# Scatter-adding weighted expert rows into the residual in memory, with gathers six blocks ahead and a copy at the end

## The reference

```python
x = L0_attn_x                                   # 8 x 512 x 512
x = x + 0.5 * ffn(layernorm(x))
x = x + attention(layernorm(x))                 # 16 heads, ALiBi bias, causal
x = x + 0.5 * ffn(layernorm(x))

def ffn(h, gate, up, down, topk_idx, topk_weight):   # E = 32 experts, K = 4 per token
    perm = argsort(topk_idx.reshape(-1))
    tok = repeat(arange(n), K)[perm]
    g, u = ragged_dot(h[tok], gate), ragged_dot(h[tok], up)
    o = ragged_dot(silu(g) * u, down) * topk_weight.reshape(-1)[perm][:, None]
    return zeros(n, 512).at[tok].add(o)
```

## Time and profile before

| | |
|---|---|
| median of 3 runs | 3252.62 us (3252.36 to 3259.63) |
| profiled execution, its own time | 3253.32 us |
| span of the trace | 3251.6 us |
| busy share of the span | PE 83%, PE weight load 60%, DVE 50%, ACT 40%, POOL 34% |
| moved by transfers | 434.78 MB, 134 GB/s over the span |

### The profile page before, as it was taken

How to read it: one execution, slowest core, us unless ns; L and a number is a source line. 1 busy time by engine, 2 the same in 40 slices (tenths; PEclk the granted TensorE clock), 3 DMA queues, 4 the chain that set the end, 5 groups by cost and what they waited for, 6 DMA issues and landing times. The chain is left out here.

```text
span 3251.6 us, 65525 instructions
## 1 busy us (share of the span) xinstructions
PE 2698.2 (83%) x13668; PEld 1963.3 (60%) x13669; DVE 1631.8 (50%) x3136; ACT 1306.9 (40%) x3316; POOL 1089.8 (34%) x1529
## 2 busy tenths in 40 slices
PE   1259999999992799999899999986899999999800
PEld 0148887888881455555555555553788788888700
DVE  8754444544433364654646465542444445454245
ACT  1235555555542222322322232221555555555422
POOL 2435555555541000100110001001455555455456
PEclk9999999999996788888897888886999999999955
DMA  2335444455403344343434434320455455543088
GB/s 71 129 123 173 163 160 154 173 175 173 151 13 116 94 112 118 98 129 93 130 93 122 114 91 127 79 79 36 154 175 172 150 167 173 178 158 110 1 322 298
DMA packets 153904, 434.78 MB, mean 134 GB/s; under 512 B 30993, under 2 KB 32529, under 8 KB 141538
## 3 DMA queue, kind: packets, MB, share of 16 engines
q1 hardware_dynamic: 95520, 282.25, 27.9%
q0 software_dynamic: 55936, 151.10, 13.9%
q10 hardware_dynamic: 2370, 0.64, 0.1%
HBM read 290.10 MB, written 125.83 MB: 128 GB/s over the span
## 5 line engine op out<-in xcount | busy, mean ns | idle before, releaser
L430 PE MATMUL f_psg<-f_wh,f_xh 128*128 x1280 | 563.5, 440 | 17.0 <-DVE f_idle L575 9.1
L430 PE MATMUL f_psg<-f_wh,f_xl 128*128 x1280 | 505.8, 395 | 0.0
L430 PE MATMUL f_psg<-f_wl,f_xh 128*128 x1280 | 504.1, 394 | 0.0
L380 POOL DMA_INDIRECT f_xg<-xn_rows,f_it x320 | 337.4, 1054 | 264.9 <-POOL f_it L377 264.0
L388 POOL DMA_INDIRECT y_rows<-f_ob,f_ip x320 | 329.5, 1030 | 284.6 <-POOL f_ip L385 253.3
L1219 DVE TENSOR_REDUCE a_mx<-a_psa 128x1 f32<-128x128 f32 (+3 forms) x512 | 237.6, 488 | 243.4 <-PE a_psa L983 234.6
L569 DVE TENSOR_TENSOR f_wl<-f_wraw,f_wh 128x768 f32 x256 | 244.9, 959 | 200.0 <-ACT f_wh L494 199.9
L582 DVE TENSOR_TENSOR f_xl<-f_psx,f_xh 128x512 fp32r<-128x512 f32 x320 | 221.0, 691 | 210.7 <-ACT f_xh L505 203.9
L505 ACT ACTIVATE f_xh<-f_psx 128x512 fp32r<-128x512 f32 x320 | 191.3, 598 | 264.4 <-PE f_psx L417 256.2
L1124 ACT ACTIVATE a_pt<-a_psb 128x256 f32<-128x256 f32 (+3 forms) x512 | 208.6, 436 | 193.1 <-PE a_psb L1032 188.4
L430 PEld LDWEIGHTS f_psg<-f_wh,f_xh 128*128 128x128 f32 x1280 | 242.5, 189 | 65.4 <-issue 35.0
(11 more groups left out here) (163 smaller groups left out, 4819.3 us busy)
## 6 DMA issues: line engine op xcount, KB each, us to landing
f_wraw<-w_in SPq DMA_DIRECT2D x64, 1536.0 KB, 7.2
a_y<-y_rows SPq DMA_DIRECT2D x128, 256.0 KB, 3.8
z_y<-y_rows SPq DMA_DIRECT2D x32, 1024.0 KB, 7.2
a_stq<-a_qk SPq DMA_DIRECT2D x128, 192.0 KB
a_stk<-a_qk SPq DMA_DIRECT2D x128, 192.0 KB
r_xt<-x_in SPq DMA_DIRECT2D x32, 256.0 KB, 4.3
xn_rows<-r_xo SPq DMA_DIRECT2D x32, 256.0 KB, 3.0
a_xt<-x_in SPq DMA_DIRECT2D x8, 1024.0 KB, 8.0
```

The lines of the kernel that those rows point to most:

```text
L380: g.indirect_dma_start(xg[:, j, :], None, xn_d, bass.IndirectOffsetOnAxis(it[:, j:j + 1], 0), bounds_check=tok_max, oob_is_err=False).then ...
L430: mm = pe.matmul(psg[:, j, :], x[:, j, k, :], w[:, cols], start=(k == 0 and n == 0), stop=(k == DC - 1 and n == 2))
```

## The change

1. `final` becomes one transfer from the memory of the second residual to the output.
2. The scatters of `moe` add to the residual in memory (`compute_op=ALU.add`) instead of writing rows of `y_rows`. The routing weight is applied by ACT in `result`, as its scale. The weights travel with the gathered rows: `xn_rows` has 32 columns more, one for each expert, that `route` fills. Two scatters of one expert never name the same token; those of different experts can. So `go` on SP lets a scatter start once the scatter two blocks earlier has landed, and at a new expert once the one before it has landed too.
3. A token that names an expert twice has the second pair removed and both weights added up in `route` ("twin").
4. Unused rows go to 256 spare rows behind the residual and are added there.
5. The gathers have four buffers and are issued six blocks ahead of the scatter beside them, with the index columns of four blocks copied at once; the outputs have four buffers.
6. In PE's turn `turn_h` of the block before stands beside `turn_x`, and `down` ends the turn. `product_high` and `product_low` move to the start of the next turn of ACT and DVE.
7. `attend` reads the finished residual: `sums`, `load_rows` and `store_x1` are gone.
8. `route` copies x into the residual's memory, from ACT's queue.

```diff
 def route
+                # DVE, ahead of the one-hot masks: 7 instructions on at most 128x128 that mark twins
+                ch.step(v.scalar_tensor_tensor(idxf[:, :], again, float(2 * E), idxf[:, :], ALU.mult, ALU.add))
...
+                v.wait_ge(s_tin, 32)
+                ch.step(v.tensor_copy(tidxf[:, :], tidx[:, :]))
+                v.tensor_tensor(weq[:, :, :], tidxf[:, :].unsqueeze(2).to_broadcast([P, NT * K, E]),
+                                row(E).unsqueeze(1).to_broadcast([P, NT * K, E]), ALU.is_equal).then_inc(s_weq, 1)
...
+                ch.step(v.scalar_tensor_tensor(pos[:, :], again, float(2 * NB * P), pos[:, :], ALU.mult, ALU.add))
...
             @block.scalar
+                a.dma_start(tidx[:, :].rearrange("p (t k) -> p t k", k=K),
+                            idx_d.rearrange("a (b k) -> (a b) k", k=K).rearrange("(t p) k -> p t k", p=P)
+                            ).then_inc(s_tin, 16)
+                a.dma_start(twk[:, :], wk_d).then_inc(s_tin, 16)
+                a.dma_start(x1_d[0:T, :].rearrange("(p r) n -> p (r n)", p=P),
+                            x_d.rearrange("(p r) n -> p (r n)", p=P)).then_inc(s_init, 16)
...
+                a.wait_ge(s_wd, 5)
+                a.dma_start(xn_d[:, D:XROW].rearrange("(t p) e -> p t e", p=P), wd[:, :, :]).then_inc(s_init, 16)
...
             @block.gpsimd
+                g.wait_ge(s_weq, 1)
+                ch.step(g.tensor_tensor(weq[:, :, :], weq[:, :, :],
+                                        twk[:, :].unsqueeze(2).to_broadcast([P, NT * K, E]), ALU.mult))
+                ch.step(g.tensor_tensor(wd[:, :, :], part[:, :, 0, :], part[:, :, 1, :], ALU.add))
+                ch.step(g.tensor_tensor(wd[:, :, :], wd[:, :, :], part[:, :, 2, :], ALU.add))
+                ch.step(g.tensor_tensor(wd[:, :, :], wd[:, :, :], part[:, :, 3, :], ALU.add))
...
 def moe
+                def go(b, r):
+                    if below(b, OB + 1):
+                        if b:
+                            sp.wait_ge(s_sca[(r + OB - 1) % OB], landed(b - 1, (r + OB - 1) % OB))
+                    else:
+                        want = sp.value_load(blk[0:1, 3, ds(b, 1)], min_val=0, max_val=16 * (NB // OB))
+                        sp.wait_ge(s_sca[(r + OB - 1) % OB], want)
+                        sp.sem_inc(s_spare_s, 1)
+                    if not below(b, 2):
+                        sp.wait_ge(s_sca[(r + OB - 2) % OB], landed(b - 2, (r + OB - 2) % OB))
+                    sp.sem_inc(s_go, 1)
+                for b in range(2 * NS):
+                    go(b, b % NS)
+                    load(b + AHEAD, (b + AHEAD) % NS)
...
                 def scatter(b, n):
                     g.wait_ge(s_ob, b + 1)
+                    g.wait_ge(s_go, b + 1)
+                    g.indirect_dma_start(x_d, bass.IndirectOffsetOnAxis(it[:, n:n + 1], 0), ob[:, n % OB, :], None,
+                                         compute_op=ALU.add).then_inc(s_sca[n % OB], 16)
...
+                    for n in range(IB):
+                        b = i * IB + n
+                        if n % XB == 0:
+                            fetched = indices(b, n, i * (IB // XB) + n // XB)
+                        scatter(b - LAG, (n + IB - LAG) % IB)
+                        gather(b, n, fetched)
...
                 def turn(b, r):
                     j = r % 2
-                    gate_up(b, j, (0, 1))
+                    gate_up(b, j, r, (0, 1))
+                    if not below(b, 1):
+                        turn_h(b - 1, 1 - j)
                     if there(b + 1):
-                        turn_x(b + 1, 1 - j)
-                    gate_up(b, j, (2, 3))
+                        turn_x(b + 1, 1 - j, (r + 1) % XB)
+                        find_slot(b + 1, (r + 1) % NS)
+                    gate_up(b, j, r, (2, 3))
                     if not below(b, 1):
-                        down(b - 1, 1 - j)
-                    if there(b + 1):
-                        find_slot(b + 1, 1 - j)
-                    turn_h(b, j)
+                        down(b - 1, 1 - j, (r + 3) % NS)
...
+                    a.activation(wcol[:, r:r + 1], xg[:, r, ds(e + D, 1)], ACT.Copy)
...
+                    a.activation(ob[:, r, :], pso[:, j, :], ACT.Copy,
+                                 scale=wcol[:, r:r + 1]).then_inc(s_ob, 1)
...
 def attend
-                        if g < 2 and not last:
-                            sums(b + 1, range(g * NY // 2, (g + 1) * NY // 2))
-                sums(0, range(NY))
...
 def final
+                sp.dma_start(out_d.rearrange("(p r) n -> p (r n)", p=P),
+                             d["x2"][0:T, :].rearrange("(p r) n -> p (r n)", p=P)).then_inc(s_out, 16)
+                sp.wait_ge(s_out, 16)
```

353 lines of the change are left out of this document (152 added, 201 removed).

## The result

The changed kernel takes 3144.72 us (median of 4 runs, 3142.97 to 3147.74) against 3253.55 of before in the same runs: ratio 0.9666, 95% interval 0.9653 to 0.9679, faster. The forecast was 3090, its range ended at 3142. The sum of the forecast was -163 us, the measured difference -109.

The account below looks back on a forecast made before the run. Took DVE to bound `route`, PE both `moe` pieces, PE in turns with DVE `attend`, bytes `final`. Terms -115 - 32 - 28 + 12.5, rounded -163, from 3253.3 gave 3090 us; range 3052 to 3142.

Parts of the forecast that it names:

- the prediction's own signs of being wrong: `result` or POOL's scatters waiting for landings in most experts, last transfer over 60 us, or turns keeping a 4.95 mean.
- final, 42 us: Last piece: a memory-to-memory copy of 42 us replaces 156.7 us, -115 us; the copy alone between 23.8 and 47.5.
- moe, the loop edge, -18 a piece: PE in `moe`: the excess over 4.83 us turns, mostly at hardware loop edges, is won, 18 us a piece.
- moe, the low half, +2 a piece: `down` needs the low half of hidden rows; 0.6 us slack, eaten in turns before a new expert: +2 us a piece.
- the 30 named as its bound: Low half in `moe` with no cover at all: 0.3 to 0.5 us in half of the turns, 30 us a piece.
- moe, the chain of scatters, 0 below L = 9.7 us: `go` in `moe`: two landings of time L per expert fit in 19.3 us, so waits cost nothing below 9.7 us.
- The loop edge stays and the new order stalls: Rival in `moe`: the -18 a piece are lost and some 2 come on top, 3130 us; 15%.
- The chain binds PE: Rival at `go` in both `moe` pieces: mean landing 13 us, 6.7 us for each of 64 experts, 3519 us; 7%.
- attend, -28: `attend`: 17 us of sums ahead of the first batch go, plus 11 us of PE's waits in seven batches.
- the fourth rival: Clock stays up in `attend`: 3 us less in each of seven batches, 3069 us; 8%.
- route, +12.5: `route`: DVE's added work ahead of its loop +7, small pieces beside loads +2, tail +3.5; from +9 to +25.
- POOL alone: `route`: POOL's weight columns just hidden at nothing, but 22 us if POOL had to do it alone.

Follow-up runs that it names:

- m_half: Changed kernel with weight quarters 0 (two blocks ahead) and 3 (one ahead) before `silu`, 1 and 2 behind, `result` last: 3110.9 us.
- m_start: Changed kernel, but `go` of blocks 1 to 4 waits for the landing before it only where a new expert begins: 3127.28 us.
- m_apart: Changed kernel, but scatters of four blocks in a row add into four different arrays and `go` waits for nothing: 3126.78 us.
- m_plain: Changed kernel, but the scatter stores its rows instead of adding them; the waits of `go` stay: 3113.11 us.
- m_free: Changed kernel, but the waits of `go` stand on POOL ahead of the scatter, and SP only issues weight loads: 3145.09 us.
- best: Changed kernel with m_half's order of quarters, m_start's `go`, and DVE instead of POOL making the weight columns: 3096.15 us.
- m_early: Changed kernel, but ACT and DVE handle weight quarters 0 and 2 ahead of `silu` and the product: 3638.61 us.

## Why the prediction missed

What failed are two terms of `moe`, the +2 for the low half and the nothing for the chain of scatters, the size of its -18, and the nothing for POOL's work in `route`. Two of the prediction's own signs of being wrong came: the mean turn is 5.09 us, and POOL's scatters waited for `go` 49 times in 64 experts.

- **final, 42 us.** The step of counting the bytes twice against 353 GB/s failed: 27.8 us for 8.39 MB is 302 GB/s read and 302 written at once, near the lower end of 23.8. The prediction's other estimate, 47 us if read and write share what one core gets of the memory, is not borne out either. The mechanism was right, the term came to -128.5 instead of -115.
- **moe, the loop edge, -18 a piece.** Right in kind: without other losses the short turns fall from 15.6 to 7.3 us (m_half). It was worth 8; the forecast counted all of the excess as won, the longer turns too, and these did not go.
- **moe, the low half, +2 a piece.** This failed. The slack of 0.6 us was taken as eaten by one quarter on DVE. But ACT starts quarter 0 only behind `result`, and before the change the high half of the hidden rows stood ahead of it; the chain result, quarter on ACT, quarter on DVE, low half has no slack, twice per expert. It cost 14 us a piece (21 against 7), between the 2 taken and the 30 named as its bound. The step to have made: write out ACT's order across the turn border, not DVE's alone.
- **moe, the chain of scatters, 0 below L = 9.7 us.** This failed too, and is the other half. The landings stayed within what was assumed (4.8 to 8.8 us, assumed 5 and 11). But the bound was a mean over an expert, and the code for blocks 1 to 4 of a piece waits for *every* landing before: five in a row, 29.5 us against 24.2, at the start. m_start shows some 8 us a piece for it. Of the further 3 or so over the kernel before, m_apart and m_plain show that they need both the chain and the adding; how much of them comes by late weights and how much by late gathers is open. The cover that the prediction gave the weight load behind a waiting `go` ("has a turn to spare") held in the changed kernel (m_free) and seems to be gone in the new order (best).
- **Rivals.** "The loop edge stays and the new order stalls" had 15% and 3130; its second half happened, the first not. "The chain binds PE" was priced as 6.7 us for every expert, and bound only in the first of a piece.
- **attend, -28.** The 16.8 us ahead of it went (-16.5), exactly. The 11 us for waits in seven batches failed: two waits of one batch were taken for all. The one of 1.20 us does not recur (the second profile of the same kernel has none between 0.9 and 2 us), and all of PE's waits for maxima before scores took 38.7 us before and 39.5 after. What came instead is the clock: PE was busy for 1082.58 us before and for 1056.82 after with the same 5856 matmuls, and the middle batches gained 3.5 us each. That was the fourth rival (8%, 3 us in a batch), though not for its reason, and that the term looks half right is luck. What sets the clock was not found.
- **route, +12.5.** The mask, the twins and the tail came as summed; idx landed 1.8 us later, and the mask covered a wait of 1.15. "POOL makes the weight columns meanwhile, at nothing" failed: its four instructions took 14.4 us, within the 13 to 22 of the estimate, and ended in time, but DVE stood still beside them. The 22 us for "POOL alone" was the right kind of rival for the wrong reason.

The range would have held 3145 with the 30 us a piece of the low half priced as a rival of its own (3146); the chain's start alone, 8 us a piece, would not have reached it.

## What to carry to other kernels

When an instruction is moved past a turn's border, write the queues of *all* engines around it as one chain, with the slowest case (a turn with weights), and count its slack there; a slack counted over DVE alone hid 14 us twice. Look at the first few iterations of an ordering rule by themselves: code for a prologue is often stricter than the loop's, and a backlog there is worked off slowly when the engine behind it has little to spare. Work "beside" another engine's is free only if the two may run at the same time; here GpSimd was idle for more than half of `route` and its work still cost DVE 13 us, so busy shares don't tell.

## What was not expected of the hardware

- One copy from memory to memory on one queue moves 8.39 MB in 27.8 us; reading and writing did not share the 353 GB/s that loads had reached.
- DVE and POOL excluded each other in both orders, on the shapes shown: a scan of 8.68 us stretched a POOL instruction from 7.11 to 15.33 us, and a POOL instruction of 7.11 us stretched a 0.2 us one of DVE to 6.95.
- Adding scatters cost POOL 1.61 us to issue (1.09 when storing), keep the transfer engines busy for 0.67 of the time instead of 0.44 at about the same bytes, and land in 4.8 to 8.8 us (the first five of f2).
- The granted clock in attend (the mean over its middle 700 us) was 0.87 in both profiles of the kernel before, and 0.89 to 0.91 in the changed kernel and the variants, whatever attend itself did (m_early left aside, whose attend began 236 us later).
